# One core, adaLN block with a linear-attention part and a top-2 expert part: the gate rows beside the tokens in sixteen small DMAs instead of one of 4 MB

## The reference, cut to what matters

```
sa, ca, ga, sb, cb, gb = mod[:, 0], ..., mod[:, 5]          # one row of 512 per batch
h = layernorm(x) * (1 + ca) + sa
x = x + ga * attn(h, ...)                                   # k, v, r, cumulative sum, Wo
h = layernorm(x) * (1 + cb) + sb
out0 = moe(h, router_w0, wg0, wu0, wd0)                     # top 2 of 32, SwiGLU, weighted scatter-add
out1 = moe(h, router_w1, wg1, wu1, wd1)
x = x + gb * (out0 * 2 + out1 * 2) / 4
```

## Time and profile before

| | |
|---|---|
| median of 3 runs | 5282.26 us (5280.39 to 5293.42) |
| the profiled execution's own time | 5289.94 us |
| its span, first to last instruction | 5288.2 us |
| TensorE's mean granted clock | 0.941 |
| `stage_a` | from about 57 us to about 2203 us of the span |
| `stage_c` | the rest |
| TensorE busy | 4652.6 us (88%) |
| DMA, 16 engines, mean rate | 218 GB/s over the span |

### The profile page before, as it was taken

How to read it: one execution, slowest core, us unless ns; L and a number is a source line. 1 busy time by engine, 2 the same in 40 slices (tenths; PEclk the granted TensorE clock), 3 DMA queues, 4 the chain that set the end, 5 groups by cost and what they waited for, 6 DMA issues and landing times.

```text
span 5288.2 us, 88606 instructions
## 1 busy us (share of the span) xinstructions
PE 4652.6 (88%) x22649; PEld 3834.4 (73%) x22649; DVE 3085.6 (58%) x6155; ACT 1628.1 (31%) x4045; POOL 2860.1 (54%) x2301
## 2 busy tenths in 40 slices
PE   6979797979797978288998888899999999999998
PEld 4767676767676767266776777677778888888886
DVE  6878787878787878344444444344444444444443
ACT  2333343434343433122332222233222222222222
POOL 2566666666675757434454444454545555555554
PEclk8989898989898989599999999999999999999999
DMA  5454644454445454599999999999899999899897
GB/s 209 158 140 154 148 152 139 156 139 161 139 157 136 155 146 148 129 297 313 307 300 316 292 308 266 314 309 326 198 290 236 235 257 241 232 241 235 210 237 189
DMA packets 411958, 1152.36 MB, mean 218 GB/s; under 512 B 55137, under 2 KB 55138, under 8 KB 393010
## 3 DMA queue, kind: packets, MB, share of 16 engines
q0 software_dynamic: 182512, 454.27, 36.0%
q1 hardware_dynamic: 187714, 544.26, 30.9%
q10 hardware_dynamic: 41472, 151.01, 7.5%
HBM read 719.35 MB, written 463.57 MB: 224 GB/s over the span
## 4 chain that ended last, share of the span: by engine, by line
PE 33%; DMA 17%; issue 4%; POOL 1%; DVE 1%; POOLq 0%; SPq 0%; ACT 0%; DVEq 0%; ACTq 0%
DMA out<-c_yo,c_idx 17%; PE ps L1285 10%; PE ps L1287 10%; PE ps L1286 9%; PE ps L1294 3%; PE ps L1313 1%; POOL out L1276 1%; DVE c_yo L1529 1%; POOL c_xg L1245 1%; DMA c_wt<-wsp_d 1%; POOLq L1268 0%; DVE c_xl L1517 0%; DMA wsp_d<-c_stg 0%; DVE c_hTl L1522 0%; SPq L1207 0%
## 5 line engine op out<-in xcount | busy, mean ns | idle before, releaser
L1276 POOL DMA_INDIRECT out<-c_yo,c_idx x576 | 917.3, 1593 | 1075.0 <-DMA out<-c_yo,c_idx 573.7
L1285 PE MATMUL ps<-c_wt,c_xh 128*128 128x512 f32 x2304 | 964.5, 419 | 41.8 <-issue 23.0
L1287 PE MATMUL ps<-c_wt,c_xl 128*128 128x512 f32 x2304 | 909.0, 395 | 0.0
L1286 PE MATMUL ps<-c_wt,c_xh 128*128 128x512 f32 x2304 | 904.7, 393 | 0.0
L1529 DVE SCALAR_TENSOR_TENSOR c_yo<-ps,c_wc,c_xg 128x512 f32<-128x512 f32 x576 | 432.4, 751 | 712.3 <-DMA out<-c_yo,c_idx 451.1
L1245 POOL DMA_INDIRECT c_xg<-h2g_d,c_idx x576 | 573.5, 996 | 491.2 <-DVE c_yo L1529 374.8
L1513 DVE TENSOR_TENSOR c_hh<-ps,c_sil 128x256 f32<-128x256 f32 x576 | 244.1, 424 | 827.6 <-ACT c_sil L1365 749.1
L1370 ACT CAST c_xh<-ps 128x512 fp32r<-128x512 f32 x576 | 338.0, 587 | 1088.3 <-PE ps L1294 997.9
L432 PE MATMUL ps<-xTh,wTh 128*128 128x512 f32 x1536 | 620.8, 404 | 50.7 <-DVE xTl L799 46.7
L693 POOL DMA_INDIRECT list_d<-pairs,sidx x512 | 557.4, 1089 | 199.6 <-issue 125.0
L434 PE MATMUL ps<-xTh,wTl 128*128 128x512 f32 x1536 | 607.1, 395 | 0.0
(11 more groups left out here) (196 smaller groups left out, 8023.0 us busy)
## 6 DMA issues: line engine op xcount, KB each, us to landing
c_wt<-wsp_d SPq DMA_DIRECT2D x69, 2048.0 KB
c_wt<-wsp_d SPq DMA_DIRECT2D x69, 1024.0 KB
sraw<-wex SPq DMA_DIRECT2D x194, 256.0 KB
wsp_d<-shigh SPq DMA_DIRECT2D x192, 256.0 KB
wsp_d<-sraw SPq DMA_DIRECT2D x192, 256.0 KB
c_stg<-wex ACTq DMA_DIRECT2D x96, 512.0 KB
wsp_d<-c_sgh ACTq DMA_DIRECT2D x96, 512.0 KB
wsp_d<-c_stg ACTq DMA_DIRECT2D x96, 512.0 KB
```

What stands on the lines that cost most here:

```text
L1276: nc.gpsimd.indirect_dma_start(out=out, out_offset=bass.IndirectOffsetOnAxis(ap=idx[:, n:n + 1], axis=0), in_=yo[:, n % 4, :], in_offset=N ...
L1285: nc.tensor.matmul(o, lh, rh, start=first, stop=False)
L1286: nc.tensor.matmul(o, lh, rl, start=False, stop=False)
L1287: return nc.tensor.matmul(o, ll, rh, start=False, stop=last)
```

## The change: what it does

`spread_gate` takes a part number and writes 128 rows (256 KB) instead of 2048. It is called at the head of turns 0, 2, 4 and 6 of each step, ahead of that turn's `stage_out`, so sixteen times in a batch; the call at the batch's end is gone. The final wait counts sixteen times as many increments. `store_h2` waits through the helper `gate`, which puts a wait for the constant 1 ahead of the wait for the counted value.

```diff
             def store_h2(b, s):
-                wait(sp, h2_ready, cnt(b, s, 4, 4))
+                gate(sp, (h2_ready, cnt(b, s, 4, 4)))
...
-            def spread_gate(b):
-                sp.dma_start(h2g_d[bass.ds(b * (4 * TT), 4 * TT), C:2 * C],
-                             mod_d[bass.ds(b, 1), GBH * C:(GBH + 1) * C].to_broadcast([4 * TT, C])
+            def spread_gate(b, part):
+                sp.dma_start(h2g_d[bass.ds(b * (4 * TT) + part * P, P), C:2 * C],
+                             mod_d[bass.ds(b, 1), GBH * C:(GBH + 1) * C].to_broadcast([P, C])
                              ).then_inc(gb_out, 16)
...
                 def turn(i):
                     j = s * PER_STEP + i
+                    if i % 2 == 0:
+                        spread_gate(b, s * 4 + i // 2)
                     if not (first and j == 0):
                         stage_out(b - 1 if j == 0 else b, (j - 1) % JOBS)
                     stage_in(b, j + 2)
...
                 turn(6)
-                if s == 3:
-                    spread_gate(b)
...
-            sp.wait_ge(gb_out, 16 * B)
+            sp.wait_ge(gb_out, 16 * 16 * B)
```

## The result

The changed kernel takes 5164.14 us (median of 4 runs, 5155.72 to 5175.09) where the kernel before takes 5287.84 beside it (median of 4, 5280.39 to 5299.27). The ratio is 0.9765, with a 95% interval from 0.9736 to 0.9795. That is 124 us less; 153 were forecast. A second measurement of the changed kernel, five runs beside nine of before, gave 0.9771 (0.9749 to 0.9794), 118 us by its medians. The time lies in the stated range of 5100 to 5180, but above the forecast itself, 5115 to 5150: it falls where the rival "less comes back" (5150 to 5210) has it.

A forecast was written before the change was run, and what follows sets the result against it. The bound was a stall at stage_a's seven batch boundaries, with stores queued behind a 4 MB copy. 5289.9 - 147 (boundaries) - 6 (tail) = 5137 us for the profiled execution, 5130 as median; range 5100 to 5180.

The forecast's parts named there:

- less comes back: Rival, chance 0.19: Wo jobs in GpSimd's order or the pieces cost time; only TensorE's gap is won, about 5169 us.
- What bounded the kernel: At stage_a's batch boundaries, job 27's stores stand behind the 4 MB copy; ScalarE waits 25.34 us, then GpSimd and TensorE.
- The saving per boundary, 21 us: Boundary step of stage_a: falls from 82.9 to 61.9 us, seven times, 147 us in all.
- I take 3 of the 5.2 us as staying: Boundary step: of four Wo scalings on GpSimd, 5.2 us, 3 us were expected to remain in the step's length.
- GpSimd's order is on the path in every step: Every step: TensorE waits for GpSimd's `sTl` before the output product, 4.5 us each, 25 times.
- The other way of pricing, by TensorE: Batch boundary: TensorE's 16.17 us gap goes, plus 2.9 us lost to a lowered clock; together 19 us.
- The tail, 6 us: End of stage_a: the eighth 4 MB copy fills the DMA engines and holds ScalarE's logit copy 6 us, or 0.
- The pieces hidden: Sixteen 256 KB copies per batch on SyncE's queue: 2.1 us each, within the slack, 0 on the path.
- The rule against it: The skill's advice to join small transfers: by its fit, 30 us more per batch, 240 in all, if waited for.
- The wait of `store_h2`, the first batch: An added wait for a constant long reached, and first-batch pieces beside the list fill: 0 each, the latter at most 8 us.
- Nothing comes back: Rival, chance 0.04: the copy is slow in any form and exposed pieces eat each batch's gain, about 5282 us.
- Slower: Rival, chance 0.05: each piece delays the store behind it beyond its slack, stopping ScalarE sixteen times a batch, about 5400 us.

The follow-up runs named there:

- the one-column run: The changed kernel with GpSimd's scaling of Wo cut from 512 columns to the first one: 5159.82 us, ratio 0.9725, a batch 237.33 us.
- with the scatters out of the way: The changed kernel with GpSimd's last five scatters of each step moved behind the fourth receive and lo: 5172.77 us, ratio 0.9769.
- pairs of pieces: The changed kernel with a second 256 KB copy behind each piece, to a tensor nobody reads: 5174.17 us, ratio 0.9774.

## Why the prediction was right

**What bounded the kernel.** Right. The stall of ScalarE behind the 4 MB is gone with the block, returns with the block (16 pieces at the end, 24.6 us), and does not care whether it is one DMA or sixteen.

**The saving per boundary, 21 us.** Right in kind, 2.1 us too high. A batch lost 18.9. The step that was mis-sized: "I take 3 of the 5.2 us as staying". 5.2 us stayed, against four undisturbed steps; the scaling makes 3.4 of them by the one-column run, near the 3 I took, and 1.7 have another cause. That this is also the full time of the four scalings (5.2) is chance. "GpSimd's order is on the path in every step" was too strong: with the scatters out of the way TensorE's wait for `sTl` went (one of 24 is left) and the batch stayed at 240.65. The other way of pricing, by TensorE, said 19 us and was the better one, though I did not use it: over the six batches TensorE's busy time fell by 2.0 us a batch (1316.40 to 1304.15 us, at a granted clock of 0.92 and then 0.95) and its idle time by 16.9, where 2.9 and 16.2 stood. Over the loop and its ends this is 128 us where 147 stood.

That the rest shows in the step after the marker (64.97) and not in the boundary step (58.25) is the marker's doing. In the changed kernel the x1 store at 568.96 follows the last of VectorE's x1 products at once (568.77), with one of the four scalings ahead of it and three behind. Before, the products were done at 585.05 and the store was issued only at 610.62, so what the engines did in between counts to the boundary step there, and to the step behind it now.

**The tail, 6 us.** Wrong, it is 0: the other bound that I had named. From the last x1 store to stage_c it takes 63.5 us before and 64.0 after. ScalarE's gap ahead of the copy of the logits is there with idle DMA engines; changed kernel, ScalarE and the windows of the same stretch:

```profile
2038.42 0.37 ACT L588 COPY lgt<-ps 128x256 f32<-128x256 f32 x1 [14.23 <-remote]
```

```profile
2026.00:2048.00 22.00, 6.30 (x40) 5.98 (x39) 5.95 (x37) 3.13 (x18) 8.61 (x9) 0.50 0.01 1
```

TensorE had finished the logits at 2031.4 (2024.33 and 7.06 us), and the DMA share is 0.01, so full engines are not what held it for 7 us. All fourteen profiles have such a gap between the last logits and their copy, 6.3 to 10.4 us, and the run with all copies behind the loop, with full engines there (share 1.01 from 2024 to 2035), has 6.4, one of the shortest. I had read two ends at nearly the same time as cause and effect. What holds ScalarE is open. The fetch of instructions which the Trainium skill ("Runtime: NRT & Kernel Launch", Instruction fetch mechanics) names is not shown and not ruled out: the changed kernel's trace has packets of kind "instruction", none of which starts between 2003.13 us and 2041.99, when the copy was past, but it does not say whose they are or whether it records those of ScalarE.

**The pieces hidden.** Right: 0 on the path, with all of it out of the loop as the test. "2.1 us each" was too high; some 0.9 us each by the shares, and the DMA share is 0.48 where I wanted to see 0.6. I had carried the rate of the block over to the piece.

**The rule against it.** The Trainium skill ("DMA: Bandwidth & Descriptors", Rules for kernel authors) wants small transfers joined. The runs disagree for a transfer that nobody waits for: sixteen, thirty-two or none a batch give 240.8, 240.6 and 240.7 us.

**The wait of `store_h2`, the first batch.** 0 as said. The first three x1 stores are at 155.85, 208.47 and 270.95 against 155.35, 207.95 and 270.37. The kernel with 128 copies of the row has the old wait, and its batch is 240.53, so the new one shows no more than some 0.2 us.

**The rivals.** "Less comes back" (5169, from 5150 to 5210) is the case that holds the measured 5164, and not the forecast; that the stated range held it too is because it reached 30 us past the forecast. Of the 38 us between the forecast for the profiled execution (5137) and what it took (5175), 19 are the loop's, 6 the tail's, and 13 stage_c's. The rival's mechanism was half right, GpSimd's order with Wo's jobs in it; its other half, that the pieces cost, is refuted; and it priced the boundary by TensorE's gap alone, 16.2 us, where 18.9 came back. "Nothing comes back" rested on a copy slow in any form, and it is not. "Slower" needed a delay per piece beyond its slack, and even pairs of pieces showed none.

## What to carry to other kernels

In a queue that runs in order, look at what stands behind a large transfer, not at who waits for the transfer: its price is its own time less the slack of the first thing behind it that somebody needs. Cutting it helps only if the cuts are spread between things with slack; cut in place it costs the same. And ask why it is slow: here reading the same row again and again was, and 128 copies of that row fixed it without moving anything.

## What the runs showed of the hardware that I had not expected

A copy from DRAM to DRAM that reads the same 2 KB 2048 times runs at 117 to 134 GB/s with full engines, by windows of 5 to 28 us in the kernel before; the same copy from 128 rows used sixteen times runs at 332, and from 2048 rows at 310 to 382. The slow rate is that of many such reads in a row: sixteen pieces one behind the other are as slow as the block (119 to 121 GB/s), while single pieces among other traffic took some 0.9 us of the engines' time, about 290 GB/s (an estimate from the shares 0.48 and 0.42), and a second piece right behind the first 1.7 us, about 160 (an estimate from 0.59 and 0.48).

Four float32 instructions of VectorE with two SBUF inputs took 7.74 us beside GpSimd's products, with 4.71 in the first of them, and 2.78 beside GpSimd's indirect DMAs. An order that removes a wait by moving products can cost VectorE as much.
